# A decoder layer's relative scores through DRAM: one transfer of 128 rows, or four of 32

## The chip, the cores and the metric

One NeuronCore of a Trainium2 chip runs the whole program. The metric is the device time of one execution in microseconds (us); less is better. Times before come from three plain runs and one execution under the hardware profiler.

## The reference

Inputs are `x` and `ctx`, both (4, 1024, 512) in float32: four batch rows, S = 1024 positions, width 512. Three sublayers follow one another, each with a residual and a layer norm:

- self-attention, 16 heads of width 64, with a bias by distance;
- cross-attention over `ctx`, 16 heads of width 32, causal, with relative scores (below);
- a mixture of 16 experts, each of which takes the 128 tokens it weighs highest, three matrix products deep.

The change touches the relative scores alone:

```python
QEr = einsum('bhsd,ld->bhsl', q, Er)      # every query row times all 1024 distance rows
Srel = _skew(QEr)                         # row i is moved so that column j holds distance i - j
attn = (q @ k.T + Srel) / sqrt(32)
attn = softmax(where(tril, attn, -inf))   # key j > row i is masked
```

For a query row i only keys j <= i count, so only columns S-1-i to S-1 of its row of `QEr` are ever used.

## The kernel before, in words

The four batch rows go one after the other: a hardware loop over three of them and an unrolled last one. A batch row has a self-attention stage (some 300 us), a projection stage, a stage that makes relative scores, and a stage of cross-attention. The experts come once, after all four.

Cross-attention cuts the 16 heads into four groups `qd` of four heads (HPQ = 4, DH = 32) and the 1024 query rows into eight tiles `t` of 128. Tile t needs `width(t)` = 128(t+1) columns w.

**Making relative scores.** There are XV = 32 tiles v per batch row, for each group in the order t = 7, 6, ... 0. For each tile TensorE makes 512-column chunks for the four heads (`relative`, L1485), between them pieces of later projections (`project_eighth`, L1455 and L1465). ScalarE copies heads 0 and 1 from PSUM (`copy_rel`, L835) and VectorE heads 2 and 3 (L1094) into one of three SBUF buffers, `relb[v % 3]`, which lie over `pts`, `wct` and `big`. When both have copied the whole tile, SyncE (SP) stores it to `skew_d` in DRAM (L579). The copies of tile v wait until the store of tile v-3 has landed (`rel_stored[v % 3]`). TensorE begins a chunk when both copies of the chunk before are done.

**The skew.** A row of w columns is stored at pitch w and read back at pitch w-1 from element P-1 on, so that row p arrives moved by P-1-p columns. That access pattern is the whole skew:

```python
at = skew_d[v, P * w * heads[0] + P - 1:P * w * heads[0] + P]
src = bass.AP(tensor=at.tensor, offset=at.offset, ap=[[w - 1, P], [P * w, nh], [1, w]])
sp.dma_start(skw[u % 4]...[:, :, 0:w], src).then_inc(skew_loaded[u % 4], 16)
```

**Using them.** Cross-attention runs NU = 48 units u per batch row: tiles t < 4 with four heads, tiles t >= 4 as two units of two heads. `load_skewed(u)` (L570) fills one of four buffers `skw[u % 4]` and is issued once VectorE has finished unit u-4 (`max_ready`). GpSimd masks the future in each (`mask_future`, L677), and then VectorE adds the scores from PSUM and takes the row maximum (`add_relative`, L1112); ScalarE's exponentials (L714), TensorE's transposes (L1550) and the weighing (L1565) follow. The loads of units 0 and 1 are issued early, after tile 15 is stored; all others only after the last stores have been waited for. SP's queue is one list in program order. Between the loads stand `load_swapped` (L590, four transfers of 64 partitions), and from unit 26 on the loads of the next batch row (`xt`, weights, bias tables; L438, L443, L468).

Two other transfers are spoken of below: `spread_v` (L458), which copies `v` within SBUF in sixteen transfers of 32 partitions and 128 KB, and the load of the distance table `er_sb` from DRAM (L657, GpSimd's queue), four transfers of 32 partitions and 128 KB each into partitions 0-31, 32-63, 64-95 and 96-127.

Of the kernel before, what the change touches and what calls it, by code (L numbers as in the profile page):

```python
# [23 lines left out]
P = 128  # L24
S, D = 1024, 512
DC = D // P
ST = S // P
# [9 lines left out]
DH = 32  # L37
QUADS = HEADS * DH // P
HPQ = P // DH
# [4 lines left out]
EARLY = 2  # L44
TABLE_PARTS = {3: [(S + 3 * P, TOEP)], 6: [(S, S + 3 * P)], 7: [(S - P, S), (0, S - P)]}
GROUPS = P // DH
KB = S // DH
XT = HPQ * ST
XV = QUADS * ST
# [10 lines left out]
NU = len(UNITS)  # L60
# [25 lines left out]
def decoder_layer(nc, x, xT, cT, wqkv, wo, rel, onehot, wx, bv, erT, wg, bg, w1, b1, w2, b2, w3, b3,  # L86
# [3 lines left out]
    with ExitStack() as ctx:  # L90
# [6 lines left out]
        skew_d = dram("skew_d", [XV, HPQ * P * S])  # L97
# [82 lines left out]
        rel_stored = [sem(f"rel_stored{i}") for i in range(3)]  # L180
        swap_loaded = [sem(f"swap_loaded{i}") for i in range(3)]
        skew_loaded = [sem(f"skew_loaded{i}") for i in range(4)]
# [222 lines left out]
        def ot_on_dve(u, v):  # L405

            return u < NU and len(UNITS[u][2]) == HPQ and not halved(v)

        def halved(v):

            return ST // 2 <= v % ST < ST - 1
# [23 lines left out]
        def _(sp):  # L435
# [46 lines left out]
            def batch(b, last=False):  # L482
# [77 lines left out]
                def load_skewed(u):  # L560

                    qd, t, heads = UNITS[u]
                    v, w, nh = qd * ST + t, width(t), len(heads)
                    if u >= 4:
                        sp.wait_ge(max_ready, FIRST[u - 3])
                    made = qd * ST + REL_ORDER.index(t)
                    sp.wait_ge(rel_stored[made % 3], 16 * (made // 3 + 1))
                    at = skew_d[v, P * w * heads[0] + P - 1:P * w * heads[0] + P]
                    src = bass.AP(tensor=at.tensor, offset=at.offset, ap=[[w - 1, P], [P * w, nh], [1, w]])
                    sp.dma_start(skw[u % 4].rearrange("p (h n) -> p h n", h=nh)[:, :, 0:w], src  # L570
                                 ).then_inc(skew_loaded[u % 4], 16)

                for v in range(XV):
                    t = REL_ORDER[v % ST]
                    w = width(t)
                    made = NCH * (v // ST) + max(j for j in range(NCH) if CHUNKS[j][0] == t) + 1
                    sp.wait_ge(rel_by_act, made)
                    sp.wait_ge(rel_by_dve, made)
                    sp.dma_start(skew_d[v - v % ST + t, 0:HPQ * P * w].rearrange("(h p n) -> p h n", h=HPQ, p=P),  # L579
                                 relb[v % 3][:, :, 0:w]).then_inc(rel_stored[v % 3], 16)  # L580
                    if v == 2 * ST - 1:
                        load_skewed(0)
                        load_skewed(1)
                sp.wait_ge(rel_stored[2], 16 * len(range(2, XV, 3)))

                def load_swapped(qd):

# [4 lines left out]

                for u in range(2, NU):
                    if u == 4:
                        sp.wait_ge(rel_stored[1], 16 * len(range(1, XV, 3)))
                        load_swapped(0)
                    load_skewed(u)
                    if u in (5, 7):
                        load_swapped((u - 3) // 2)
                    if u == NU // 2:  # L600
                        load_swapped(3)
                    if last:
                        if u == PRELOAD[0]:
                            for free in (w_free, *table_free):
                                sp.wait_ge(free, 1)
                            for n, w in enumerate((w1, w2)):
                                sp.dma_start(w_front[n], w[0].rearrange("(c p) n -> p c n", p=P)).then_inc(we_loaded[n], 16)
                        continue
                    if u == PRELOAD[0]:
                        sp.wait_ge(xt_free, 1)  # L610
                        sp.sem_inc(xt_free, -1)
                        load_xt(b + 1)
                    if u == PRELOAD[1]:
                        sp.wait_ge(w_free, 1)
                        sp.sem_inc(w_free, -1)
                        load_wqk(0)
                        load_wv(0)
                    if u in PRELOAD[2:]:
                        i = PRELOAD[2:].index(u)
                        sp.wait_ge(table_free[i], 1)  # L620
                        sp.sem_inc(table_free[i], -1)
                        load_table(0, i)
# [1 line left out]
                sp.wait_ge(x2_ready, 1)  # L624
                sp.sem_inc(x2_ready, -1)
                for i in range(3):
                    sp.sem_inc(rel_stored[i], -16 * len(range(i, XV, 3)))
                def store_rows(dst):

                    sp.dma_start(dst[bass.ds(b * S, S), :].rearrange("(t p) d -> p t d", p=P), xr[:, :, :]  # L630
# [22 lines left out]
        @block.gpsimd  # L653
        def _(pool):
            with nc.allow_non_contiguous_dma(reason="small constants"):
                for dst, src in CONSTS:
                    pool.dma_start(dst, src).then_inc(const_loaded, 16)  # L657
            def scale_probs(k):

                pool.wait_ge(sums_inverted, k + 1)  # L660
                pool.tensor_scalar(sc[k % 4][:, :], sc[k % 4][:, :], pinv[:, k % 4:k % 4 + 1], 1.0,  # L661
                                   ALU.mult, ALU.mult).then_inc(probs_scaled, 1)

            def batch(last=False):

                with pool.Fori(0, PAIRS):
                    for k in range(TP):
                        scale_probs(k)
                    pool.sem_inc(sums_inverted, -TP)

                def mask_future(u):

                    _, t, heads = UNITS[u]
                    pool.wait_ge(skew_loaded[u % 4], 16 * (u // 4 + 1))
                    near = skw[u % 4].rearrange("p (h n) -> p h n", h=len(heads))[:, :, P * t:P * t + P]

                    pool.affine_select(out=near, in_=near, compare_op=ALU.is_ge, fill=-BIG, base=0,  # L677
                                       pattern=[[0, len(heads)], [-1, P]], channel_multiplier=1
                                       ).then_inc(masked, 1)

                def add_output(v):

                    pool.wait_ge(ot_scaled, v + 1)
                    cols = xr[:, v % ST, P * (v // ST):P * (v // ST) + P]
                    pool.tensor_tensor(cols, o_part[:, v % 4, :], cols, ALU.add).then_inc(x_added, 1)

                for u in range(NU + 6):
                    if u < NU:
                        mask_future(u)
                    if last and u == NU // 2:  # L690
                        pool.wait_ge(picks_done, 1)
                        pool.wait_ge(xt_free, 1)
                        for b in SOONER:
                            pool.indirect_dma_start(tok[:, b, :], None, x2_d[0:S * len(SOONER), :],
                                                    bass.IndirectOffsetOnAxis(ap=rows[:, b, 0:1], axis=0)
                                                    ).then_inc(step_gathered[b], 16)
                    for v in range(XV):
                        if LAST[v] + 5 == u:
                            add_output(v)
                for i in range(4):  # L700
                    pool.sem_inc(skew_loaded[i], -16 * (NU // 4))

            with pool.Fori(0, B - 1):
                batch()
            batch(last=True)

        @block.scalar
        def _(act):
# [51 lines left out]
            def batch(last=False):  # L760
# [67 lines left out]
                def copy_rel(qd, j):  # L828

                    t, n = CHUNKS[j]  # L830
                    v, m = qd * ST + REL_ORDER.index(t), min(HALF, width(t) - n)
                    act.wait_ge(rel_for_act, NCH * qd + j + 1)
                    if v >= 3:
                        act.wait_ge(rel_stored[v % 3], 16 * (v // 3))
                    act.copy(relb[v % 3][:, 0:2, n:n + m], psum[:, 4:6, 0:m]).then_inc(rel_by_act, 1)  # L835

                root_of_variance()
# [28 lines left out]
                    k = FIRST[u] + i  # L866
                    exp_tile(k, scx[u % 2][:, span(u, i)], xmax[:, k:k + 1], xsum[:, k:k + 1])

                act.wait_ge(rel_stored[0], 16 * len(range(0, XV, 3)))
                for u in range(NU + 4):  # L870
                    for v in range(XV):
                        if LAST[v] + 3 == u and not ot_on_dve(u, v):
# [28 lines left out]
        def _(dve):  # L901
# [86 lines left out]
            def batch(last=False):  # L988
# [98 lines left out]
                def copy_rel(qd, j):  # L1087

                    t, n = CHUNKS[j]
                    v, m = qd * ST + REL_ORDER.index(t), min(HALF, width(t) - n)  # L1090
                    dve.wait_ge(rel_for_dve, NCH * qd + j + 1)
                    if v >= 3:
                        dve.wait_ge(rel_stored[v % 3], 16 * (v // 3))
                    dve.tensor_copy(relb[v % 3][:, 2:4, n:n + m], psum[:, 6:8, 0:m]).then_inc(rel_by_dve, 1)  # L1094

                copy_block(1)
# [41 lines left out]
                                      OTURNED.rearrange("p (h d) -> p h d", h=HPQ), scale, ALU.mult  # L1138
                                      ).then_inc(ot_scaled, 1)

                dve.wait_ge(rel_stored[0], 16 * len(range(0, XV, 3)))
                def row_stats(t):

                    dve.wait_ge(x_added, XV - ST + t + 1)
# [1114 lines left out]
```

## Time and profile before

| | us |
|---|---|
| median of 3 runs | 4080.67 (4078.1 to 4083.45) |
| profiled execution | 4071.49 |
| its span | 4069.7 |
| PE busy / DVE / ACT / POOL | 3828.7 / 2471.1 / 1598.8 / 897.9 |
| DMA moved | 671.68 MB, mean 165 GB/s |

The span is the time from the first to the last instruction seen by the profiler. PE is TensorE's matmul, PEld its weight load, DVE VectorE, ACT ScalarE, POOL GpSimd, SP SyncE; a q behind a name is that engine's sequencer, which waits, branches and issues transfers. "DMA share" is the mean busy share of the core's 16 DMA engines, GB/s what they moved, and PEclk the share of TensorE's full clock that was granted.

### The profile page before, as it was taken

How to read it: one execution, taken by the hardware profiler on the slowest of the kernel's cores; microseconds unless marked ns; L12 is line 12 of the kernel's file. 1: busy time of each engine (PE TensorE's matmuls, PEld its weight loads, DVE VectorE, ACT ScalarE, POOL GpSimd, SP SyncE). 2: the span in 40 equal slices, each digit the busy share in tenths (PEclk: the TensorE clock that was granted, in tenths of full speed). 3: DMA queues.
4: the chain of work that ended last, by engine and by line, in shares of the span. 5: the costliest groups of instructions: out<-in, count | busy, mean ns of one | idle time of the engine just before them, and what ended most of it. 6: DMA issues, size and time to landing. Idle time of an engine off the chain costs nothing. (4 is left out here: it accounts for less than half of the span.)

```text
span 4069.7 us, 91371 instructions
## 1 busy us (share of the span) xinstructions
PE 3828.7 (94%) x37104; PEld 2365.1 (58%) x37104; DVE 2471.1 (61%) x4870; ACT 1598.8 (39%) x3247; POOL 897.9 (22%) x1005
## 2 busy tenths in 40 slices
PE   5999999989999999899999999999999989999997
PEld 2676644656776546566764465676644655544445
DVE  3777535877776358777773487888734873122224
ACT  2444324854443147544431376444413862100002
POOL 2333200213332002133330021333300212222221
PEclk8999999999999999999999999999999999999998
DMA  8333439744334397443342985433429855666666
GB/s 260 104 93 93 141 136 333 259 141 118 94 95 135 115 340 264 157 118 92 97 124 113 327 270 176 112 97 97 124 93 334 274 175 147 157 154 152 152 151 186
DMA packets 317182, 671.68 MB, mean 165 GB/s; under 512 B 27841, under 2 KB 120753, under 8 KB 313665
## 3 DMA queue, kind: packets, MB, share of 16 engines
q1 hardware_dynamic: 276096, 617.85, 47.5%
q0 software_dynamic: 15024, 34.41, 4.6%
q10 hardware_dynamic: 25664, 13.77, 1.4%
q8 instruction: 292, 4.78, 0.5%
q14 instruction: 106, 0.86, 0.1%
HBM read 383.40 MB, written 210.04 MB: 146 GB/s over the span
## 5 line engine op out<-in xcount | busy, mean ns | idle before, releaser
L714 ACT ACTIVATE sc<-sc,nmax 128x1024 f32<-128x1024 f32 x512 | 587.0, 1147 | 775.8 <-DVE nmax L952 775.4
L661 POOL TENSOR_SCALAR sc<-sc,pinv 128x1024 f32<-128x1024 f32 x512 | 572.1, 1118 | 1174.8 <-DVE pinv L960 1161.5
L952 DVE CUSTOM_DVE_ANT_0 sc<-psum,w_and_tables 128x1024 f32<-128x1024 f32 x512 | 603.6, 1213 | 97.9 <-PE psum L1267 81.7
L1325 PE MATMUL psum<-pts,wct 32*64 32x256 f32 x8192 | 460.0, 376 | 8.3 <-PEq L1320 4.6
L1325 PE MATMUL psum<-xall,wct 32*64 32x256 f32 x8192 | 460.5, 376 | 6.6 <-issue 6.5
L1310 PE MATMUL psum<-xt,w_and_tables 128*128 128x256 f32 x1792 | 415.7, 385 | 23.0 <-PEq L1307 23.0
L1112 DVE CUSTOM_DVE_ANT_0 sc<-psum,big 128x896 f32<-128x896 f32 (+7 forms) x512 | 364.2, 754 | 101.4 <-PE psum L1536 86.2
L1310 PEld LDWEIGHTS psum<-xt,w_and_tables 128*128 128x128 f32 x1792 | 332.5, 190 | 127.7 <-issue 66.3
L714 ACT ACTIVATE sc<-sc,xmax 128x896 f32<-128x896 f32 (+7 forms) x512 | 395.0, 773 | 11.7 <-DVE xmax L1112 11.6
L977 DVE STREAM_TRANSPOSE pts<-sc 128x1024 f32<-128x1024 f32 (+3 forms) x340 | 331.2, 974 | 109.5 <-PE psum L1325 67.4
L1325 PEld LDWEIGHTS psum<-pts,wct 32*64 32x64 f32 x8192 | 309.5, 132 | 98.3 <-issue 53.5
L677 POOL TENSOR_SCALAR_AFFINE_SELECT big<-big 128x256 f32<-128x256 f32 (+1 forms) x192 | 92.7, 483 | 1150.8 <-DMA big<-skew_d 1150.8
L1325 PEld LDWEIGHTS psum<-xall,wct 32*64 32x64 f32 x8192 | 324.4, 131 | 17.1 <-issue 12.3
L977 DVE STREAM_TRANSPOSE xall<-sc 128x1024 f32<-128x1024 f32 (+3 forms) x340 | 324.4, 954 | 2.3 <-POOL sc L661 0.8
L1550 PE MATMUL psum<-ident,sc 128*128 128x128 f32 x2304 | 311.9, 280 | 6.6 <-ACT sc L714 5.6
L1550 PEld LDWEIGHTS psum<-ident,sc 128*128 128x128 f32 x2304 | 257.2, 142 | 77.3 <-DVE pts L1122 39.8
L1267 PE MATMUL psum<-xall 64*128 64x512 f32 x1024 | 261.7, 630 | 22.4 <-ACTq L713 10.3
L1297 PEld LDWEIGHTS psum<-w_and_tables,xt 128*128 128x128 f32 x2048 | 236.3, 192 | 75.4 <-issue 75.4
L1892 ACT ACTIVATE hid<-psum,bias 128x128 f32<-128x128 f32 (+1 forms) x80 | 34.3, 431 | 594.1 <-PE psum L2112 554.7
L1267 PE MATMUL psum<-big,xall 64*128 64x512 f32 x1024 | 254.4, 615 | 10.2 <-ACTq L713 8.1
L1297 PE MATMUL psum<-w_and_tables,xt 128*128 128x128 f32 x2048 | 254.5, 280 | 0.6 <-PEq L1295 0.5
L1536 PE MATMUL psum<-xall 32*128 32x512 f32 (+3 forms) x1024 | 204.1, 589 | 46.7 <-DVE xmax L1112 34.2
(221 smaller groups left out, 5191.2 us busy)
## 6 DMA issues: line engine op xcount, KB each, us to landing
wct<-xall SPq DMA_DIRECT2D x576, 128.0 KB, 2.4
big<-skew_d SPq DMA_DIRECT2D x48, 1024.0 KB, 5.5
big<-skew_d SPq DMA_DIRECT2D x48, 768.0 KB, 4.5
w_and_tables<-rows_d SPq DMA_DIRECT2D x64, 448.0 KB, 5.1
big<-skew_d SPq DMA_DIRECT2D x32, 896.0 KB, 4.9
w_and_tables<-w_dram SPq DMA_DIRECT2D x26, 1024.0 KB, 5.8
big<-skew_d SPq DMA_DIRECT2D x32, 640.0 KB, 7.0
w_and_tables<-wqkv_dram SPq DMA_DIRECT2D x32, 512.0 KB, 3.7
```

Source lines behind the costliest of these rows:

```text
L661: pool.tensor_scalar(sc[k % 4][:, :], sc[k % 4][:, :], pinv[:, k % 4:k % 4 + 1], 1.0, ALU.mult, ALU.mult).then_inc(probs_scaled, 1)
L677: pool.affine_select(out=near, in_=near, compare_op=ALU.is_ge, fill=-BIG, base=0, pattern=[[0, len(heads)], [-1, P]], channel_multiplier=1 ...
L714: act.activation(tile, tile, ACT.Exp, bias=least, scale=-1.0, accum_out=total).then_inc(probs_ready, 1)
L952: dve.tensor_tensor_reduce(sc[k % 4][:, :], SLOT[h], table[h][:, off:off + S], -1.0, BIG, ALU.add, ALU.min, nmax[:, k % 4:k % 4 + 1]).then ...
L977: ins = dve.transpose(probs_t(h, t, first, last), tile[:, first:last, :])
L1112: dve.tensor_tensor_reduce(scx[u % 2][:, at], SCORES[:, at], skw[u % 4][:, at], -XSCALE, BIG, ALU.add, ALU.min, xmax[:, k:k + 1]).then_inc ...
L1267: mm = pe.matmul(psum[:, 2 * h + n, :], qf[which][HEAD[h], P * t:P * t + P], kf[which][HEAD[h], HALF * n:HALF * n + HALF], start=True, sto ...
L1297: mm = pe.matmul(SPARE[m // 2][:, P * (m % 2):P * (m % 2) + P], xt[:, c, P * m:P * m + P], w_sb[:, 2, c, :], start=(c == 0), stop=(c == DC ...
L1310: mm = pe.matmul(SPARE[m], w_sb[:, a, c, :], xt[:, c, QG * m:QG * m + QG], start=(c == 0), stop=(c == DC - 1))
L1325: mm = pe.matmul(OSUM[HEAD[h], a, :], v_all[rows, ST * (b % GROUPS) + b // GROUPS, HEAD[h]], ptf[h][rows, QG * b:QG * b + QG], start=(b == ...
L1536: mm = pe.matmul(SCORES[:, at:at + m], q, k, start=True, stop=True)
L1550: mm = pe.transpose(TURN[m % 3][:, P * (i % 4):P * (i % 4) + P], scx[u % 2][:, at:at + P], ident[:, :])
```

## The change

Each tile's 128 rows are cut into four bands of 32. The last row of band g (rows 32g to 32g+31) begins at column P-1-(32g+31) = 96-32g, the first column that any row of the band reads; the columns before it, `skip` = 96, 64, 32, 0, are no longer stored. Each band is stored with its own pitch m = w - skip, behind the bands before it, and loaded at pitch m-1 from element 31 on. So a store is four transfers of 32 partitions, and so is a load; all four add to the same semaphore, and every wait on it now asks for 64 where it asked for 16. Columns m to w of a band stay unwritten in the destination; the mask fills them.

```diff
+BANDS = [(DH * g, P - DH - DH * g) for g in range(GROUPS)]
+STORED = 16 * len(BANDS)
...
-                    sp.wait_ge(rel_stored[made % 3], 16 * (made // 3 + 1))
-                    at = skew_d[v, P * w * heads[0] + P - 1:P * w * heads[0] + P]
-                    src = bass.AP(tensor=at.tensor, offset=at.offset, ap=[[w - 1, P], [P * w, nh], [1, w]])
-                    sp.dma_start(skw[u % 4].rearrange("p (h n) -> p h n", h=nh)[:, :, 0:w], src
-                                 ).then_inc(skew_loaded[u % 4], 16)
+                    sp.wait_ge(rel_stored[made % 3], STORED * (made // 3 + 1))
+                    for (row, skip), start in zip(BANDS, band_starts(w)):
+                        m = w - skip
+                        first = start + DH * m * heads[0] + DH - 1
+                        at = skew_d[v, first:first + 1]
+                        src = bass.AP(tensor=at.tensor, offset=at.offset, ap=[[m - 1, DH], [DH * m, nh], [1, m]])
+                        sp.dma_start(skw[u % 4].rearrange("p (h n) -> p h n", h=nh)[row:row + DH, :, 0:m], src
+                                     ).then_inc(skew_loaded[u % 4], 16)
...
-                    sp.dma_start(skew_d[v - v % ST + t, 0:HPQ * P * w].rearrange("(h p n) -> p h n", h=HPQ, p=P),
-                                 relb[v % 3][:, :, 0:w]).then_inc(rel_stored[v % 3], 16)
+                    for (row, skip), start in zip(BANDS, band_starts(w)):
+                        m = w - skip
+                        sp.dma_start(skew_d[v - v % ST + t, start:start + HPQ * DH * m]
+                                     .rearrange("(h p n) -> p h n", h=HPQ, p=DH),
+                                     relb[v % 3][row:row + DH, :, skip:w]).then_inc(rel_stored[v % 3], 16)
...
-                    pool.wait_ge(skew_loaded[u % 4], 16 * (u // 4 + 1))
+                    pool.wait_ge(skew_loaded[u % 4], STORED * (u // 4 + 1))
...
-                        act.wait_ge(rel_stored[v % 3], 16 * (v // 3))
+                        act.wait_ge(rel_stored[v % 3], STORED * (v // 3))
```

VectorE's waits change like ScalarE's. No instruction of TensorE, VectorE, ScalarE or GpSimd is added or moved; SP's list grows from 351 rows to 861.

The first stores of a batch row on SP's queue. Before, partitions x heads x columns:

```order
L579 DMA skew_d<-pts 128x4x1024
L579 DMA skew_d<-wct 128x4x896
L579 DMA skew_d<-big 128x4x768
L579 DMA skew_d<-pts 128x4x640
L579 DMA skew_d<-wct 128x4x512
```

With the change:

```order
L591 DMA skew_d<-pts 32x4x928
L591 DMA skew_d<-pts 32x4x960
L591 DMA skew_d<-pts 32x4x992
L591 DMA skew_d<-pts 32x4x1024
L591 DMA skew_d<-wct 32x4x800
L591 DMA skew_d<-wct 32x4x832
L591 DMA skew_d<-wct 32x4x864
L591 DMA skew_d<-wct 32x4x896
```

Each store has become four on the same queue, one band after the other; the tiles' order is the same.

The first loads of cross-attention that follow the last store on the same queue, units 2, 3 and 4. Before:

```order
L570 DMA big<-skew_d 128x4x384
L570 DMA big<-skew_d 128x4x512
L590 DMA wct<-xall 64x512 x4
L570 DMA big<-skew_d 128x2x640 x2
L590 DMA wct<-xall 64x512 x4
```

With the change:

```order
L580 DMA big<-skew_d 32x4x288
L580 DMA big<-skew_d 32x4x320
L580 DMA big<-skew_d 32x4x352
L580 DMA big<-skew_d 32x4x384
L580 DMA big<-skew_d 32x4x416
L580 DMA big<-skew_d 32x4x448
L580 DMA big<-skew_d 32x4x480
L580 DMA big<-skew_d 32x4x512
L603 DMA wct<-xall 64x512 x4
L580 DMA big<-skew_d 32x2x544
L580 DMA big<-skew_d 32x2x576
```

The swapped rows (64 partitions) still stand behind unit 3, now behind eight transfers instead of two.

## Rows read from the trace of the kernel before

**Rows 1.** The page: busy time by engine, and the DMA's 40 slices.
```profile
PE 3828.7 (94%) x37104; PEld 2365.1 (58%) x37104; DVE 2471.1 (61%) x4870; ACT 1598.8 (39%) x3247; POOL 897.9 (22%) x1005
...
DMA  8333439744334397443342985433429855666666
GB/s 260 104 93 93 141 136 333 259 141 118 94 95 135 115 340 264 157 118 92 97 124 113 327 270 176 112 97 97 124 93 334 274 175 147 157 154 152 152 151 186
```

**Rows 2.** Windows (start:end, length; busy us and count by engine; PEclk, DMA share, GB/s).
```profile
576.00:580.00 4.00, 4.00 (x21) 1.56 (x22) 1.92 (x2) 2.61 (x3) 0.00 (x0) 1.00 1.01 401
600.00:622.00 22.00, 21.68 (x114) 8.20 (x114) 10.17 (x11) 8.57 (x11) 0.00 (x0) 1.00 0.99 378
563.00:684.00 121.00, 114.51 (x680) 54.02 (x678) 53.46 (x59) 42.40 (x53) 1.27 (x2) 0.99 0.86 320
...
684.00:859.00 175.00, 159.94 (x2018) 106.26 (x2022) 143.15 (x397) 140.62 (x352) 35.03 (x76) 0.98 0.76 253
```

**Rows 3.** First and last start of L1485 in 563:684 and of L1112 in 563:859.
```profile
L1485 PE MATMUL psum<-er_sb,xall x384: 270/586/692, 563.8 to 679.3; 32*128 32x512 f32 x96, 32*128 32x384 f32 x32, 32*128 32x256 f32 x32, 32*128 32x128 f32 x32
...
L1112 DVE DVE_READ_ACCUMULATOR2_ANT xmax<- x128: 80/83/86, 683.6 to 858.7; 128x1 f32 x128
```

**Rows 4.** Timeline of SP: stores of one group of heads (start us, us).
```profile
569.34 0.38 SPq L579 DMA_DIRECT2D skew_d<-pts  x1
574.82 0.38 SPq L579 DMA_DIRECT2D skew_d<-wct  x1
...
590.88 0.36 SPq L579 DMA_DIRECT2D skew_d<-pts  x1
592.74 0.36 SPq L579 DMA_DIRECT2D skew_d<-wct  x1
598.40 0.36 SPq L579 DMA_DIRECT2D skew_d<-big  x1
```

**Rows 5.** Waits of VectorE on stores, 563:684 (us in total, times, longest).
```profile
DVE wct L1094 <- DMA skew_d<-wct: 6.3, 4, 1.9
...
DVE big L1094 <- DMA skew_d<-big: 3.3, 2, 1.8
...
DVE pts L1094 <- DMA skew_d<-pts: 2.8, 2, 1.6
```

**Rows 6.** Timeline: unit 3 and unit 16, masked by GpSimd, then added by VectorE.
```profile
692.09 0.63 POOL L677 TENSOR_SCALAR_AFFINE_SELECT big<-big 128x512 f32<-128x512 f32 x1 [3.12 <-DMA big<-skew_d]
...
692.86 0.69 DVE L1112 CUSTOM_DVE_ANT_0 sc<-psum,big 128x512 f32<-128x512 f32 x1 [0.90 <-PE psum L1536]
...
734.17 0.41 POOL L677 TENSOR_SCALAR_AFFINE_SELECT big<-big 128x256 f32<-128x256 f32 x1 [2.98 <-DMA big<-skew_d]
...
741.14 0.82 DVE L1112 CUSTOM_DVE_ANT_0 sc<-psum,big 128x640 f32<-128x640 f32 x1
```

**Rows 7.** Windows of two stretches in which transfers of 32 partitions run.
```profile
917.00:925.00 8.00, 8.00 (x36) 5.55 (x34) 7.28 (x14) 4.95 (x9) 2.74 (x3) 1.00 0.91 206
14.00:17.00 3.00, 0.01 (x1) 0.04 (x1) 0.00 (x0) 0.00 (x0) 0.00 (x0) 1.00 1.04 232
```

**Rows 8.** Timelines of SP and GpSimd: the issues of these transfers.
```profile
915.17 10.22 SPq L458 DMA_DIRECT2D wct<-xall  x16
...
4.95 2.05 POOL L657 DMA_DIRECT2D er_sb<-erT_dram  x4
```

**Rows 9.** Windows around the end of the stage of relative scores.
```profile
678.00:681.00 3.00, 1.54 (x19) 1.23 (x16) 1.57 (x3) 0.96 (x2) 0.00 (x0) 1.00 1.03 365
681.00:684.00 3.00, 0.81 (x8) 0.55 (x8) 1.31 (x6) 0.25 (x1) 0.00 (x0) 0.63 1.01 286
684.00:692.00 8.00, 7.64 (x40) 4.04 (x44) 4.72 (x24) 7.42 (x26) 0.63 (x1) 0.50 1.02 298
```

**Rows 10.** DMA issues in 684:859: KB each, us to landing.
```profile
big<-skew_d SPq DMA_DIRECT2D x11, 1024.0 KB, 5.3
...
wct<-xall SPq DMA_DIRECT2D x16, 128.0 KB, 7.9
xt<-xT_dram SPq DMA_DIRECT2D x1, 2048.0 KB, 9.9
```

More of the change, by code:

```diff
@@ L407, in ot_on_dve, with band_starts @@
             return u < NU and len(UNITS[u][2]) == HPQ and not halved(v)
+        def band_starts(w):
+            sizes = [HPQ * DH * (w - skip) for _, skip in BANDS]
+            return [sum(sizes[:g]) for g in range(len(BANDS))]
         def halved(v):
@@ L583, in batch @@
                         load_skewed(1)
-                sp.wait_ge(rel_stored[2], 16 * len(range(2, XV, 3)))
+                sp.wait_ge(rel_stored[2], STORED * len(range(2, XV, 3)))
                 def load_swapped(qd):
@@ L594, in batch @@
                     if u == 4:
-                        sp.wait_ge(rel_stored[1], 16 * len(range(1, XV, 3)))
+                        sp.wait_ge(rel_stored[1], STORED * len(range(1, XV, 3)))
                         load_swapped(0)
@@ L626, in batch @@
                 for i in range(3):
-                    sp.sem_inc(rel_stored[i], -16 * len(range(i, XV, 3)))
+                    sp.sem_inc(rel_stored[i], -STORED * len(range(i, XV, 3)))
                 def store_rows(dst):
@@ L700, in batch @@
                 for i in range(4):
-                    pool.sem_inc(skew_loaded[i], -16 * (NU // 4))
+                    pool.sem_inc(skew_loaded[i], -STORED * (NU // 4))
             with pool.Fori(0, B - 1):
@@ L867, in xexp @@
                     exp_tile(k, scx[u % 2][:, span(u, i)], xmax[:, k:k + 1], xsum[:, k:k + 1])
-                act.wait_ge(rel_stored[0], 16 * len(range(0, XV, 3)))
+                act.wait_ge(rel_stored[0], STORED * len(range(0, XV, 3)))
                 for u in range(NU + 4):
@@ L1092, in copy_rel @@
                     if v >= 3:
-                        dve.wait_ge(rel_stored[v % 3], 16 * (v // 3))
+                        dve.wait_ge(rel_stored[v % 3], STORED * (v // 3))
                     dve.tensor_copy(relb[v % 3][:, 2:4, n:n + m], psum[:, 6:8, 0:m]).then_inc(rel_by_dve, 1)
@@ L1139, in scale_output @@
                                       ).then_inc(ot_scaled, 1)
-                dve.wait_ge(rel_stored[0], 16 * len(range(0, XV, 3)))
+                dve.wait_ge(rel_stored[0], STORED * len(range(0, XV, 3)))
                 def row_stats(t):
```

## The prediction

> **What bounds the kernel now.** I read the page first. TensorE is busy for 94% of the span [rows 1], so in most of the program a transfer costs nothing. The DMA's slices show where that fails: at the same place of every batch row two slices stand out, 333 and 259 GB/s, then 340 and 264, 327 and 270, 334 and 274, while their neighbours move 90 to 160 [rows 1]. This is the stage that stores the relative scores and the start of the one that loads them.
>
> The windows of one batch row come next. Between 600 and 622 us the 16 DMA engines are busy for 99% of the time and move 378 GB/s; the best stretch has 401 [rows 2]. TensorE is busy for 114.5 of the stage's 121 us. So here TensorE and DMA are nearly equal bounds, with the DMA at full rate. The stage runs from the first relative matmul at 563.8 to the first addition at 683.4, one L1112 before its first read-out at 683.6: 119.6 us [rows 3]. VectorE already waits 6.3 + 3.3 + 2.8 = 12.4 us for buffers that a store has not yet left [rows 5]. Cross-attention then takes 175 us, up to 858.7, with a DMA share of 0.76 at 253 GB/s [rows 2, 3]. Its loads have a short lead at first: unit 3 is masked at 692.1 and used at 692.9, while unit 16 is masked at 734.2 and used at 741.1 [rows 6].
>
> **What the change removes.** A tile has 4 heads x 128 rows x 4 bytes = 2048 bytes for each column. The eight widths sum to 4608 columns, and the mean skip is (96+64+32+0)/4 = 48, so they become 4224. Per batch row that is 4 x 4608 x 2048 = 37.7 MB stored before and 34.6 MB after, and the same for the loads: 8.3% less. At 378 GB/s this is 8 us of transfer in each stage; it could save only what now waits, at most the 12.4 us above.
>
> **What it adds: issues.** One issue occupies SP for 0.36 us [rows 4], so a tile costs 1.44 instead of 0.36. The narrowest tiles follow one another in 1.86 us (590.88 to 592.74), the widest in 5.5 (569.34 to 574.82), so this fits. I cost it at nothing; if every issue took the 0.64 us of L458 (10.22 / 16) [rows 8], a tile would need 2.6 us, which only the two narrowest of a group exceed, about 1 us each, 8 us per batch row at most. But while the DMA itself is late, SP is ahead of it and this is hidden.
>
> **What it adds: narrow transfers.** This decides. The trace has no narrow store to DRAM, so I bound the rate from both sides. The upper end is what full-height stores reach, 378 GB/s [rows 2]. The lower end is two stretches of narrow transfers. From 917 to 925 us sixteen 32-partition copies within SBUF run: share 0.91, yet only 206 GB/s. From 14 to 17 us, after GpSimd has queued the four bands of `er_sb` from DRAM, the share is 1.04 and the rate 232 GB/s [rows 7, 8]. In both the engines are busy all the time and move just over half the bytes: something other than the number of bytes fills them. The second case is the nearest to the change: DRAM to SBUF, four bands in partition order in one queue. That it also includes other loads makes it an upper guess for bands alone. I take 215 GB/s for stores and loads, between 206 and 232, and keep both ends. That the four bands lie side by side in the queue does not help in the second case, so I give no credit for it.
>
> The Trainium skill has a rule here, in "SBUF — State Buffer", section "Door 1: The DMA port swizzle": rows 0-31, and 0-63 as well, reach only 8 of SBUF's 16 DMA ports, and it gives 189 GB/s at 1 MiB against 328 for 128 rows. By 189 the sum below would be +456 instead of +292; the rows of this case are faster, and they are what I use.
>
> **Relative stage.** I replayed the 32 tiles with three buffers: the copies of tile v start when those of v-1 are done and the store of v-3 has landed, a wide tile takes 5.5 us to make, a narrow one 1.5 to 1.9 [rows 4]. With 375 GB/s and one transfer each the replay gives 121.4 us, against 119.6 in the trace. With bands at 215 it gives 179.8. By hand: 5.5 us until the first tile is made, 34.6 MB / 215 = 161, 0.6 MB for the loads of units 0 and 1 = 2.7, 1.6 to land the last, and about 3 us at each of the three borders between groups. There the two narrowest tiles (590 KB, 2.8 us) are all that the queue holds while a tile of 5.5 us is made. Sum 180. The stage grows by **58 us**. Ends: at 232 by 47, at 206 by 65.
>
> **Cross-attention.** Loads must fit beside 175.4 us of work. The same replay with four buffers, a load being issued when the addition of unit u-4 is done, gives 174.6 before and 189.4 at 215 GB/s: **+15 us**. By hand: 34.0 MB of scores at 215 = 158 us, 2.1 MB of swapped rows [rows 10] at the same rate 10, and about 4.8 MB of `xt`, weights and tables at 343 = 14, together 182; some 7 us of idle queue remain because a load cannot be issued earlier than four units ahead. The covering work (VectorE's and TensorE's) is used up. Ends: +8 at 232, +19 at 206. The border between the stages is in both terms.
>
> **Clock.** Before, TensorE was busy for 2.35 us of the six from 678 to 684, and then its granted clock fell to one half, 1.2 GHz instead of 2.4, until about 692 [rows 9]. Afterwards each wide tile needs 2.0 MB / 215 = 9.3 us of transfer and 5.5 of making, so TensorE stands still for 3.8 us a tile. Some drops will come; while the DMA is late they mostly cost nothing, since 11 us at half speed is only 1.7 more than 9.3. I add 5 us per batch row.
>
> **Sum.** 58 + 15 + 5 = 78 us per batch row, four of them: 312. The profiled execution took 4071.5, so 4384. The median of the runs is 9 us higher, 4080.7, so I forecast 4392. Outside the two stages nothing changes.
>
> **The rivals.**
>
> *Faster: full rate is kept* (0.10). If what slowed the two stretches was copying within SBUF in the one, and a mixture of queues in the other, then bands move at 375. The replay gives -4 us per batch row in the first stage and 0 in the second, where the lead suffices: 4064 for the median. With issues of 0.55 us nothing is left of it: 4081. It decides from about 340 GB/s on, where the replay gives +9 in all. For it: 401 GB/s shows that the engines have more in them. Against it: a share of 1.04 at 232 [rows 7] with transfers from DRAM. I split it 0.07 faster, 0.03 within 0.2%, which is 8 us and about what a measurement of this kernel can tell.
>
> *Halves overlap in part* (0.12). When some engines are already at bands of the other half of the partitions, the rate lies at 250 to 300. The replay gives +37 and +3 at 250, +15 and 0 at 300: 4141 to 4241.
>
> *The clock becomes the bound* (0.12). If TensorE is at half clock in half of the relative stage, the work of 114.5 us becomes 172, no longer well hidden under 180: I estimate 20 to 25 us more per batch row, 4470 to 4490. For it: TensorE would be busy for 64% of the stage, in pieces. Against it: in [rows 9] the clock fell after 2.35 us of work in six, and here it would be 5.5 in 9.3.
>
> *Narrower still* (0.06). Pieces of 128 to 512 bytes, and stores that start at odd multiples of 128 bytes, could bring it to 165 to 189 GB/s: 4540 to 4750.
>
> *Main case* (0.60): 206 to 232 GB/s, 4302 to 4436. The low end is +222 + 0 for the clock, the high end +336 + 20, on 4080.7.
>
> **Range and chances.** 4230 to 4540 holds the main case, the clock's case and the edges of the neighbours, about 0.8. Slower by over 0.2%: 0.12 + 0.12 + 0.06 + 0.60 = 0.90; within 0.2% 0.03; faster 0.07.
>
> **What would show it.** In the DMA slices the two high slices per batch row become three or so at a share of 9 and some 210 GB/s. The windows of the relative stage show a share near 1.0 at 200 to 230 GB/s and TensorE busy for about two thirds. VectorE's and ScalarE's waits on stores rise from 12 to some 60 us per batch row. Between first relative matmul and first addition lie 180 us, and cross-attention takes 185 to 195, with additions that wait for GpSimd's mask. Bytes on the SP queue fall by 25 MB. The forecast is wrong if the share is below 0.8 in that stage, or the rate above 250 GB/s; a rate as forecast with a longer stage would point to the clock or to SP's issues.

## The result and the profile after

| | before | changed |
|---|---|---|
| median, us | 4080.88 | 4332.22 (4 runs, 4321.02 to 4336.66) |
| ratio | 1 | 1.0612 (95%: 1.0589 to 1.0634) |
| profiled execution, us | 4071.49 | 4329.13 |

The change makes the kernel 251 us slower; the forecast was 4392, 311 slower.

The page of the changed kernel, with the same lines as [rows 1] and TensorE's granted clock ahead of them:

```profile
PE 3926.1 (91%) x37104; PEld 2427.3 (56%) x37104; DVE 2472.0 (57%) x4870; ACT 1603.4 (37%) x3247; POOL 897.5 (21%) x1005
...
PEclk8999997999999989999999889999997899999998
DMA  7433268964334489743343898343428995466666
GB/s 251 117 92 92 98 161 219 224 151 113 95 94 131 114 220 231 178 118 92 92 131 92 214 217 198 110 110 102 116 77 213 223 215 166 117 153 158 155 144 186
```

The two slices at 333 and 259 GB/s have become two at 219 and 224, at a share of 8 and 9 tenths, and the slices beside them rose to 161 and 151. The clock shows dips (7, 8) in the same slices. DVE and POOL have the same busy time to within 1 us; PE has 97 us more at the same number of instructions. The bytes fell by 25 MB, from 671.68 to 646.64.

Windows of the first batch row: the whole relative stage and the whole of cross-attention, which answer to the last two of [rows 2], then pieces of the first store stream:

```profile
563.00:730.00 167.00, 130.29 (x680) 62.87 (x678) 52.93 (x54) 42.31 (x52) 1.27 (x2) 0.85 0.82 211
730.00:926.00 196.00, 170.93 (x2018) 114.44 (x2022) 143.90 (x401) 142.02 (x352) 34.90 (x76) 0.91 0.96 211
...
571.00:574.00 3.00, 3.00 (x17) 1.20 (x14) 1.27 (x2) 1.11 (x2) 0.00 (x0) 1.00 0.98 201
576.00:579.00 3.00, 3.00 (x17) 1.29 (x14) 1.37 (x2) 2.23 (x3) 0.00 (x0) 1.00 0.98 208
583.00:584.00 1.00, 1.00 (x10) 0.34 (x6) 0.42 (x1) 0.37 (x1) 0.00 (x0) 1.00 0.83 303
...
607.00:609.50 2.50, 2.50 (x21) 1.72 (x21) 1.22 (x1) 1.01 (x1) 0.00 (x0) 1.00 0.11 26
```

The rate is not one number. The share is that of the engines' time in which they are busy, so GB/s divided by the share is the rate of busy engines, called here the rate for a share of 1. Where bands of the same half of the rows follow one another, the engines are full at some 205 GB/s; within the stream there are stretches of 303 at a smaller share. Over the stage 211 GB/s at a share of 0.82 make 257 GB/s for a share of 1, in cross-attention 211 at 0.96 make 220. Between two groups of heads the DMA is nearly idle (26 GB/s) while TensorE works.

The first and last start of the additions, which answer to [rows 3]; the first relative matmul starts at 563.98 us:

```profile
L1125 DVE CUSTOM_DVE_ANT_0 sc<-psum,big x128: 278/755/1226, 730.1 to 924.6; 128x128 f32<-128x128 f32 x16, 128x256 f32<-128x256 f32 x16, 128x384 f32<-128x384 f32 x16, 128x512 f32<-128x512 f32 x16
L1125 DVE DVE_READ_ACCUMULATOR2_ANT xmax<- x128: 80/83/85, 730.3 to 925.7; 128x1 f32 x128
```

So the relative stage takes 166.1 us (119.6 before) and cross-attention 195.7 (175.4). By the same marks the four batch rows have 166.1, 163.5, 167.0, 165.8 and 195.7, 191.5, 193.5, 191.6: together 46 + 18 = 64 us more per batch row, 256 in all. Self-attention with the projections (528 us from one batch row's last addition to the next one's first relative matmul) and the experts are unchanged to 3 us.

The waits of VectorE on stores from 563 to 728 us, against [rows 5]:

```profile
DVE wct L1107 <- DMA skew_d<-wct: 25.2, 7, 4.4
...
DVE big L1107 <- DMA skew_d<-big: 21.4, 5, 5.2
...
DVE pts L1107 <- DMA skew_d<-pts: 17.7, 5, 4.4
```

64 us where 12.4 were. And the lead of the masks, in a timeline of both engines against [rows 6]:

```profile
764.36 0.41 POOL L690 TENSOR_SCALAR_AFFINE_SELECT big<-big 128x256 f32<-128x256 f32 x1 [5.34 <-DMA big<-skew_d]
...
764.91 1.09 DVE L1125 CUSTOM_DVE_ANT_0 sc<-psum,big 128x896 f32<-128x896 f32 x1 [3.73 <-POOL big L690]
```

Unit 8 is used 0.5 us after its mask begins, and VectorE has waited 3.7 us for it. Over the whole of cross-attention these waits of VectorE grow by 16.6 us, close to the 18 that the stage has grown. Before (684 to 859) and after (730 to 926):

```profile
DVE sc L1112 <- POOL big L677: 1.9, 1, 1.9
```

```profile
DVE sc L1125 <- POOL big L690: 18.5, 7, 4.5
```

### The profile page after: what moved, and what is told of

Read it like the earlier page. It is cut to its first block and busy times, and to the rows that moved or that the text cites. A ratio compares the mean times of both kernels' runs of the same rounds, so it can differ in the third digit from the quotient of the medians.

```text
span 4327.3 us, 92331 instructions
## 1 busy us (share of the span) xinstructions
PE 3926.1 (91%) x37104; PEld 2427.3 (56%) x37104; DVE 2472.0 (57%) x4870; ACT 1603.4 (37%) x3247; POOL 897.5 (21%) x1005
## 2 busy tenths in 40 slices
DMA packets 332550, 646.64 MB, mean 149 GB/s; under 512 B 55489, under 2 KB 148401, under 8 KB 329025
## 5 line engine op out<-in xcount | busy, mean ns | idle before, releaser
L1563 PE MATMUL psum<-ident,sc 128*128 128x128 f32 x2304 | 329.2, 291 | 5.7 <-ACT sc L727 4.8
L1563 PEld LDWEIGHTS psum<-ident,sc 128*128 128x128 f32 x2304 | 275.7, 149 | 76.6 <-DVE pts L1135 39.4
L1498 PE MATMUL psum<-er_sb,xall 32*128 32x512 f32 (+3 forms) x1536 | 200.7, 594 | 118.1 <-DVE big L1107 43.4
```

The costliest lines, as they stand in the source:

```text
L1498: mm = pe.matmul(psum[:, 4 + h, 0:m], xq[DH * h:DH * h + DH, qd, P * t:P * t + P], er_sb[DH * h:DH * h + DH, S - w + n:S - w + n + m], sta ...
L1563: mm = pe.transpose(TURN[m % 3][:, P * (i % 4):P * (i % 4) + P], scx[u % 2][:, at:at + P], ident[:, :])
```

## The experiments

Theory N: a transfer of 32 rows fills the 16 DMA engines at little more than half the bytes. Theory C: four transfers cost by being four. Stage times below are means over the four batch rows by the marks above. Ratios are against runs of the kernel before on the same chip.

**Four full-height transfers.** Stores cut by head, loads by head or by head and column half:

```diff
-for (row, skip), start in zip(BANDS, band_starts(w)):
-    ... relb[v % 3][row:row + DH, :, skip:w]
+for h in range(HPQ):
+    ... relb[v % 3][:, h, 0:w]
```

> Four transfers a tile as in the change, the same waits for 64, but each covers all 128 rows: stores are cut by head, loads by head or by head and half of the columns, and no column is left out. Theory N (a transfer of 32 rows fills the 16 DMA engines at about half the bytes): the loss goes, 4080 us give or take 12, relative stage about 120 us from first relative matmul to first addition, over 350 GB/s between 600 and 622 us. Theory C (four transfers cost by being four: issues, completions, a longer queue): about as slow as the changed kernel, 4330, or slower since more bytes move.

Measured: 4093.09 us, ratio 1.0034 (1.0022 to 1.0047). Relative stage 121.1 us, cross-attention 179.4.

```profile
562.00:683.00 121.00, 113.49 (x678) 53.66 (x670) 53.15 (x57) 41.38 (x51) 1.27 (x2) 0.98 0.85 320
...
600.00:622.00 22.00, 21.71 (x108) 7.36 (x100) 10.18 (x11) 8.57 (x11) 0.00 (x0) 1.00 0.96 363
```

The windows are close to those of the kernel before (320 at 0.86, 378 at 0.99). Being four costs 14 us in the whole program, mostly in cross-attention; theory C falls for the other 240.

**Bands of the whole width.**

```diff
+whole = skew_d[v - v % ST + t, 0:HPQ * P * w].rearrange("(h p n) -> p h n", h=HPQ, p=P)
+for row, _ in BANDS:
+    sp.dma_start(whole[row:row + DH], relb[v % 3][row:row + DH, :, 0:w]) ...
```

> Bands of 32 rows as in the change, but of the whole width: 37.7 MB instead of 34.6 MB per batch row each way, in the layout of the kernel before. Theory N: both stages are bound by bytes at the low rate, so 9% more bytes cost 9% of some 140 us of storing and of some 170 us of loading: 12 + 12 us per batch row, 4330 + 95 = 4425 us. Theory C: the number of transfers is the same, so 4330.

Measured: 4392.46 us, ratio 1.0767 (1.0743 to 1.0791); stages 176.6 and 199.1. Narrow transfers cost 315 us, and the change's 8.3% fewer bytes give about 60 of it back; I had expected 95. By stage, the bytes are worth 11 us in the relative stage, where 12 were expected, and 6 in cross-attention, where 12 were expected too. In this run cross-attention has a DMA share of 1.01, in the change 0.96: there the change no longer fills the engines all the time.

**Two bands of 64 rows.**

```diff
-BANDS = [(DH * g, P - DH - DH * g) for g in range(GROUPS)]
+TALL = 64
+BANDS = [(TALL * g, P - TALL - TALL * g) for g in range(P // TALL)]
```

> Two bands of 64 rows, which skip 64 and 0 columns: two transfers a tile, 3% more bytes than the change. Theory N in the form of the ports (rows 0 to 63 share the same half as rows 0 to 31): as slow as four bands or slower, 4330 to 4370. Theory N in the form that the rate goes with the number of rows: 64 rows are twice as good, no loss, 4080. Theory C: half the extra transfers, half the loss, about 4200.

Measured: 4275.84 us, ratio 1.0488 (1.0469 to 1.0507); stages 150.6 and 194.6. None of the three forms fits both stages. In cross-attention 64 rows are no better than 32 (194.6 against 193.1, with 3% more bytes). In the relative stage they are better by 15 us:

```profile
561.00:711.00 150.00, 126.51 (x679) 61.35 (x678) 52.96 (x54) 41.84 (x52) 1.27 (x2) 0.88 0.85 242
711.00:908.00 197.00, 169.60 (x2026) 112.98 (x2026) 143.95 (x401) 142.05 (x352) 35.00 (x76) 0.92 0.98 215
```

242 GB/s at 0.85 is 285 for a share of 1. Here every next transfer in the queue belongs to the other half of the rows; with four bands only every second one does. That alone does not explain the gain, since a tile has two changes of half either way, and since cross-attention gains nothing by it.

**Bands in the order 0, 2, 1, 3.** This tests just that.

```diff
-for (row, skip), start in zip(BANDS, band_starts(w)):
+for (row, skip), start in [list(zip(BANDS, band_starts(w)))[g] for g in (0, 2, 1, 3)]:
```

> The change with the bands in the order 0, 2, 1, 3, so that neighbours in the queue lie in different halves of the partitions; bytes, sizes and count are the same. If rows 0 to 63 and rows 64 to 127 are two halves with a rate of their own, engines that run ahead find the other half free at every border and not only at every second one: rate 260 to 300 GB/s instead of some 220, relative stage about 145 us, 4190 to 4260 us. If a transfer of 32 rows is slow by itself, or four are slow by being four, the order makes no difference: 4330.

Measured: 4214.98 us, ratio 1.0341 (1.0323 to 1.0358); stages 145.8 and 185.0.

```profile
563.00:709.00 146.00, 124.16 (x678) 59.37 (x678) 52.96 (x54) 41.70 (x52) 1.27 (x2) 0.91 0.80 241
709.00:892.00 183.00, 164.25 (x2010) 109.00 (x2014) 143.51 (x401) 141.26 (x351) 35.19 (x76) 0.95 0.91 227
578.00:584.00 6.00, 6.00 (x32) 2.21 (x32) 2.34 (x3) 1.97 (x3) 0.00 (x0) 1.00 0.90 309
```

The same transfers in another order lose some 110 us less by the two ratios, with 309 GB/s in the stream. I read this so: rows 0 to 63 and rows 64 to 127 have a rate of their own each, and engines that have run ahead use the other half while the rest finish the first.

The DMA packets that the traces record bear this out. A packet is one piece of a transfer, with its own size and duration in the trace. In the relative stage of the kernel before, 93% of the packets of 1000 bytes or more go at over 21 bytes per ns (median 24). In the change they are of two kinds, 49% at over 21 and 47% at under 16 (median 13), with few between. Sixteen engines at 24 bytes per ns make 384 GB/s, at 13 they make 208: the rates of [rows 2] and of one half alone. The share of slow packets goes with the length of the stage; the bands of the whole width take longer than the change at the same share because they move more bytes. All figures are of the first batch row of each run; "before" is the kernel before:

| | slow packets, relative stage | its us | slow packets, cross-attention | its us |
|---|---|---|---|---|
| before | 1% | 119.6 | 11% | 175.4 |
| four full-height transfers | 1% | 121.1 | 12% | 176.7 |
| two queues (below) | 14% | 131.0 | 69% | 190.1 |
| order 0, 2, 1, 3 | 26% | 146.0 | 45% | 182.7 |
| two bands of 64 rows | 31% | 150.0 | 77% | 196.4 |
| the change | 47% | 166.1 | 76% | 195.7 |
| bands of the whole width | 46% | 176.2 | 77% | 198.3 |

That one queue serves two bands at once can be seen too: in the order 0, 2, 1, 3 the packets of the second tile's band 0 (3200 bytes) run from 576.4 to 579.2 us and those of band 2 (3456 bytes) from 577.6 to 581.9, and 5% and 20% of them are slow. In the change bands 0 and 1 of the first tile, both in the lower half, have packets of 3712 and 3840 bytes that take 286 and 300 ns at the median; a full-height packet of 4096 bytes takes 164. Why 64-row bands keep the engines on both halves in the stores (31%) and not in the loads (77%) stays open.

**Stores on two queues.** SP issues bands 0 and 1, ScalarE bands 2 and 3, after its last copy of the tile:

```diff
+act.wait_ge(rel_by_act, NCH * qd + j + 1)
+act.wait_ge(rel_by_dve, NCH * qd + j + 1)
+for (row, skip), start in list(zip(BANDS, band_starts(w)))[2:4]:
+    ... act.dma_start(...).then_inc(rel_stored[v % 3], 16)
```

> The change, but bands 0 and 1 of each store are issued by SP and bands 2 and 3 by ScalarE, so that both halves of the partitions are served at the same time, from two queues; loads as in the change. If the two halves have a rate of their own each, the stores run at some 370 GB/s together: relative stage 117 to 125 us in place of 166, cross-attention 193 as in the change: 4332 - 4 x 44 = 4155 us. If a transfer of 32 rows is slow whatever runs beside it, the stage stays at 160 and more, 4310 us or more.

Measured: 4165.2 us, ratio 1.0221 (1.0197 to 1.0246); stages 128.1 and 189.2. The stream of [rows 2] from 600 to 622 now reads

```profile
600.00:622.00 22.00, 20.46 (x104) 7.24 (x96) 9.28 (x10) 7.62 (x9) 0.00 (x0) 1.00 1.01 318
```

The stores of both halves are now issued side by side, and 38 of the 46 us of the relative stage are gone. It is still not better than one full-height transfer: 318 GB/s against 378.

**Each side alone**, at the whole width, with the other side's transfers as before.

> Stores in four bands of 32 rows, but of the whole width; loads in one transfer as in the kernel before. whole_width had 176 us of relative stage and 199 us of cross-attention against 120 and 175. If each stage pays for its own transfers: relative stage 176 us, cross-attention 175 to 178, so 4080 + 4 x 57 = 4308 us. If the late stores also hold up the first loads, a few us more.

Measured: 4304.41 us, ratio 1.0559 (1.054 to 1.0577); stages 176.5 and 177.3.

> Loads in four bands of 32 rows of the whole width, stores in one transfer as before. Relative stage 120 us, cross-attention about 197, so 4080 + 4 x 22 = 4168 us. If the loss of cross-attention came from the stores' backlog and not from its own loads, it stays at 176 and the time at 4085.

Measured: 4167.48 us, ratio 1.0233 (1.0209 to 1.0256); stages 119.5 and 198.7.

Each stage pays for its own transfers. The two losses, 229 and 92 us, sum to 321; both together gave 315.

**The saved bytes alone.** The kernel before, full height, every row without its first 48 columns:

```diff
+m = w - CUT
+first = P * m * heads[0] + P - 1 - CUT
-    relb[v % 3][:, :, 0:w]
+    relb[v % 3][:, :, CUT:w]
```

> The kernel before, with its transfers of 128 rows, but for every row the first 48 columns are neither stored nor loaded: exactly the bytes that the change moves, at full height. It leaves out scores that rows 80 to 127 of each tile need. This prices the saved bytes alone. The replay of the relative stage gives 4 us less per batch row, and VectorE waits about 11 us per batch row for stores, of which at most that much can go: 4040 to 4066 us. If those waits only move to the end of the stage, no difference: 4075.

Measured: 4072.85 us, ratio 0.9989 (0.998 to 0.9999); stages 119.0 and 177.2. At full rate the bytes that the change saves are worth 3 us, and by the interval between 0 and 8. The stage's share falls and its length does not:

```profile
563.00:684.00 121.00, 113.58 (x682) 53.77 (x681) 53.78 (x62) 42.17 (x52) 1.27 (x2) 1.00 0.79 296
```

**TensorE's work in the relative stage, more and less.** First twice the relative matmuls of two heads:

```diff
+for h in (0, 1):
+    pe.matmul(psum[:, 4 + h, 0:m], xq[...], er_sb[...], start=True, stop=True)
 for h in range(HPQ):
     mm = pe.matmul(psum[:, 4 + h, 0:m], xq[...], er_sb[...], start=True, stop=True)
```

> The change with the relative matmuls of heads 0 and 1 done twice, into the same place: some 22 us more work for TensorE in each relative stage, which has about 35 us of idle time there, and less room for its clock to fall. If the stage is bound by the stores alone: 166 us as before it, at most 4 us more at the borders between groups, 4335 to 4350 us, PE busy 20 us more per stage. If the half clock costs the stage time, as the 14 us more of PE busy time in it suggest: PEclk in the stage rises from 0.86 towards 1 and the stage is shorter by 5 to 15 us, 4280 to 4310 us.

Measured: 4377.2 us, ratio 1.0737 (1.0718 to 1.0756); stage 178.5 us, 12.9 more than in the change.

Then fewer:

```diff
-for h in range(HPQ):
+for h in range(HPQ - 1):
+    if h == 2:
+        m = DH
```

> The change with less work for TensorE in the relative stage: head 3's relative matmul is left out and head 2's is cut to 32 columns, some 20 us per stage; the copies and all transfers stay. It leaves out the relative scores of heads 2 and 3. The run with doubled matmuls added 27 us of PE busy time and 12 us of stage. If the making of tiles decides at the borders between groups, where the stores drain, the opposite happens: stage 156 to 160 us in place of 166, 4295 to 4315 us. If the stores alone bind and the extra work merely went over what was hidden: 166 us, 4325 to 4340.

Measured: 4324.76 us, ratio 1.0605 (1.0586 to 1.0623); stage 166.2 us, as in the change. The windows of the stage, with doubled and then with fewer matmuls:

```profile
564.00:743.00 179.00, 157.03 (x870) 77.64 (x870) 53.28 (x57) 41.51 (x52) 1.27 (x2) 0.90 0.78 197
```

```profile
562.00:729.00 167.00, 134.92 (x580) 66.07 (x576) 52.99 (x55) 41.38 (x51) 1.27 (x2) 0.79 0.82 211
```

More work lengthens the stage by half of what is added (27 us of PE busy time, 12.9 of stage), so the theory "stores alone" falls for more work. Less work does not shorten it. But with 96 matmuls left out and 96 more cut short PE is busy for 134.9 us, not for less than the change's 130.3, and the granted clock is 0.79 instead of 0.85: what TensorE was spared in work came back as time at the lower clock. So this pair does not separate the clock from the stores. That the clock costs the stage some microseconds is argued, not shown.

## Why the prediction was right, and by how much it was off

*What bounds the kernel*: right. Everything happened in the two stages named, the rest moved by 3 us at most.

*Saved bytes*: "it could save only what now waits", 12.4 us per stage at most. The run at full height shows 3 us in the whole program. The rival "faster: full rate is kept", priced at 4064 to 4081, would have been real at 4073, had the rate been kept in single transfers. Four full-height transfers cost 14 us more by themselves. My estimate from the two runs is that even at the full rate the change as written would have been some 11 us slower than the kernel before.

*Issues, costed at nothing*: nearly right. Four full-height transfers, issues and all, cost 14 us. SP's issues in the changed kernel are much longer than the 0.36 us of [rows 4]:

```profile
L591 SPq DMA_DIRECT2D skew_d<-pts x176: 302/1014/2479, 569.5 to 3387.5; - x176
```

The median is 1.0 us and the longest 2.5, with the same instruction at full height in the run by head at 0.46:

```profile
L592 SPq DMA_DIRECT2D skew_d<-pts x176: 319/458/1333, 567.1 to 3159.5; - x176
```

The issues are long where the DMA is late: its share is 0.98 in the windows above. I read that as a sign of the late DMA and not as a cost by itself; no run separates the two. Two queues brought the medians back to 0.43 and 0.46 us.

*The relative stage*: right mechanism, size off. The step that failed is the credit of nothing for bands that lie side by side in the queue ("so I give no credit for it"): the term of +58 us for this stage was too large, and 46 were measured. I took 215 GB/s and +58 us; the stage ran at 257 GB/s of busy engines and +46. The run with alternating bands shows why: around each border between bands 1 and 2, and between band 3 and the next tile's band 0, engines work on both halves, and only within a half do they have 201 to 208 GB/s, near the 206 of [rows 7]. On the other side the replay with 250 GB/s gives 37 us and the stage took 46, some 9 us more. They are idle time of the DMA: a share of 0.82 over 166 us leaves 30 us idle, where my sum had 16 (5.5 for the first tile, 9 at the borders, 1.6 to land the last). The windows around the three borders between groups hold some 13 us of it instead of 9 (the last three lines):

```profile
570.50:606.00 35.50, 27.43 (x142) 13.03 (x135) 11.46 (x12) 9.59 (x12) 0.00 (x0) 0.86 0.92 239
604.00:610.00 6.00, 6.00 (x44) 4.66 (x40) 2.45 (x2) 2.02 (x2) 0.00 (x0) 0.85 0.31 77
644.00:652.00 8.00, 8.00 (x32) 2.62 (x26) 2.56 (x3) 2.20 (x3) 0.40 (x1) 0.83 0.52 127
684.00:693.00 9.00, 8.36 (x29) 3.95 (x30) 2.70 (x3) 2.40 (x3) 0.00 (x0) 0.61 0.44 114
```

The first line is the stream of the first group: its share is 0.92 and not 1, and most of the rest lies there and in the streams that follow. At the borders, the other three lines, TensorE is busy nearly all the time, partly at the lower clock. How much of either the clock causes stays open.

*The Trainium skill's rule* that rows 0 to 63 reach only 8 of 16 ports (the Trainium skill, "SBUF — State Buffer", section "Door 1: The DMA port swizzle"): no run here shows the ports, and in its effect this case agrees in part. 64 rows gave cross-attention no better time than 32, one half alone had about half of the full rate, and the order of bands mattered by half; in the relative stage 64 rows were 15 us better than 32. By the page's 189 GB/s the prediction's estimate was +456 us against 251 measured: within one half the rate here was 201 to 208, and transfers to the two halves do overlap within one queue. The Trainium skill also says, on the same page in the section "Can I just issue two DMAs to hit both halves?", that two such transfers at once gain only 6%; here the relative stage fell from 165.6 to 128.1 us when the halves were issued by two engines, at 318 GB/s where one half alone had 201 to 208, and the measurement decides.

*Cross-attention*: +15 forecast, +18 measured; 220 GB/s for a share of 1 was close to the 215 taken. The covering work was used up as expected: VectorE waits 18.5 us for masks where it waited 1.9.

*Clock*: I gave it 5 us per batch row. In the changed stage PE is busy for 130.3 us where it was for 114.5 with the same matmuls. Windows at the end of the first group show a drop:

```profile
591.00:595.00 4.00, 0.77 (x10) 0.37 (x9) 1.65 (x2) 0.80 (x1) 0.00 (x0) 1.00 0.98 248
596.00:605.00 9.00, 6.23 (x30) 3.97 (x30) 1.55 (x3) 1.45 (x3) 0.00 (x0) 0.50 0.92 251
```

TensorE waits for the stores and works 0.77 us of four, then its clock is at 1.2 GHz while the DMA is busy for 92% of the time. The work at half clock goes on beside a busy DMA, as forecast; how much of it is hidden is not shown. The rival "the clock becomes the bound" did not come: the stages sum to 64 us, not 98 and more.

*The sum*: 58 + 15 + 5 = 78 against 46 + 18 = 64. The chance of 0.60 stood on the case at 206 to 232 GB/s, 4302 to 4436 us, and the result lies in it, for the loads by its rate and for the stores only by its time: their rate, 257 GB/s, belongs to the rival "halves overlap in part", whose price of 4141 to 4241 us the result misses. That the time still fell into the main case is partly luck: too low a rate for the stores and too little idle time of the DMA went against each other. Two signs did not come as written: the share of the relative stage is 0.82 and not near 1.0, and TensorE is busy for 78% of it, not for two thirds.

No correct version here beats the kernel before. The nearest is four full-height transfers at 1.0034.

## What to carry to other kernels

Before cutting a transfer by rows to save bytes, compute what the saved bytes are worth where the time is lost: here 8.3% of the bytes were worth 3 us at full height, and cutting the transfers by rows cost 315. In a profile, a DMA share near 1 at little more than half the usual GB/s was the mark of narrow transfers here; look for one that is already in the trace before you add more. If narrow transfers can't be avoided, put neighbours in different halves of the 128 rows, or issue the halves from two engines: here the loss fell from 251 us to 137 by the one and to 90 by the other.

## What was not expected of the hardware

- The order of the same transfers in one queue was worth some 110 us: a ratio of 1.0612 in the order 0, 1, 2, 3 and of 1.0341 in the order 0, 2, 1, 3.
- Packets of the same size went at one of two speeds, about 24 or about 13 bytes per ns and engine, and the slow ones came with bands of one half in a row.
- Leaving out TensorE work in a stage that waits for DMA did not lower its busy time: 134.9 us with 96 of 384 relative matmuls left out and 96 cut short, at a granted clock of 0.79, against 130.3 us at 0.85.
- An SP issue held its sequencer for up to 2.5 us in the changed kernel, where the DMA is late, against at most 0.43 for the same stores before.
